# Attention scores on TensorE by row group: masks and product of one group in a row

## What is computed

```python
x = x + attention(layernorm(x), ctx, ctx, mask, ...)   # scores, softmax, values, wo
x = x + ffn(layernorm(x), ...)                          # router, top 2 of 8 experts, shared expert

scores = einsum('bhqd,bhkd->bhqk', Qh, Kh) / sqrt(8)
scores = where(causal or padding, -inf, scores)
probs  = softmax(scores, axis=-1)
```

## Time and profile before

| what | value |
|---|---|
| median of three runs | 856.8 us |
| lowest, highest | 856.01, 857.17 us |
| span of the profiled execution | 887.9 us |
| TensorE matmul, weight loads | 792.5 us (89%), 536.7 us (60%) |
| VectorE | 635.1 us (72%) |
| ScalarE | 638.0 us (72%) |
| GpSimd | 539.8 us (61%) |

### The profile page before, as it was taken

How to read it: one execution, slowest core, us unless ns; L and a number is a source line. 1 busy time by engine, 2 the same in 40 slices (tenths; PEclk the granted TensorE clock), 3 DMA queues, 4 the chain that set the end, 5 groups by cost and what they waited for, 6 DMA issues and landing times.

```text
span 887.9 us, 21709 instructions
## 1 busy us (share of the span) xinstructions
PE 792.5 (89%) x6977; PEld 536.7 (60%) x6977; DVE 635.1 (72%) x1774; ACT 638.0 (72%) x1185; POOL 539.8 (61%) x634
## 2 busy tenths in 40 slices
PE   5799999989999999999885747999999999967994
PEld 2355555545555555555454536888888888866773
DVE  5756667778687777856664547787777778756897
ACT  3478887877877777876596636988888888858730
POOL 6456665787878788776465743056666565644531
PEclk9899999999999999999898867999999999989998
DMA  4542643352222222211001113667777788773983
GB/s 123 163 141 86 201 127 112 108 164 60 68 72 74 65 74 82 68 59 49 29 20 58 46 69 110 240 218 257 249 246 262 248 293 288 269 227 108 249 232 106
DMA packets 100934, 126.97 MB, mean 143 GB/s; under 512 B 20919, under 2 KB 82039, under 8 KB 94807
## 3 DMA queue, kind: packets, MB, share of 16 engines
q1 hardware_dynamic: 92183, 107.08, 38.3%
q0 software_dynamic: 8640, 18.50, 5.9%
HBM read 77.84 MB, written 39.64 MB: 132 GB/s over the span
## 4 chain that ended last, share of the span: by engine, by line
PE 66%; DVE 9%; ACT 8%; issue 7%; another core or an unknown queue 4%; POOL 3%; SPq 1%; DMA 1%; ACTq 0%; DVEq 0%; POOLq 0%
PE bank L1344 8%; PE bank L1329 6%; ACT prob L760 5%; PE bank L1426 5%; PE bank L1424 5%; PE bank L1435 5%; PE bank L1437 5%; PE bank L1436 5%; PE bank L1425 5%; PE bank L1349 3%; PE bank L1361 3%; PE bank L1322 3%; PE bank L1443 2%; PE bank L1411 2%
## 5 line engine op out<-in xcount | busy, mean ns | idle before, releaser
L760 ACT ACTIVATE prob<-bank,padb,sc 120x512 f32<-120x512 f32 x256 | 178.1, 776 | 80.5 <-PE bank L1349 64.6
L1210 POOL DMA_INDIRECT y_scratch<-yo,ti x142 | 141.1, 993 | 131.2 <-DVE yo L1111 99.2
L1188 POOL TENSOR_SCALAR_AFFINE_SELECT prob<-prob 120x512 f32<-120x512 f32 x256 | 161.7, 635 | 86.2 <-ACT prob L760 80.6
L832 DVE TENSOR_REDUCE nm<-bank 128x4 f32<-128x480 f32 x256 | 150.2, 648 | 66.9 <-PE bank L1329 66.9
L1088 DVE TENSOR_TENSOR gl<-gf,gh 128x512 fp32r<-128x512 f32 (+1 forms) x220 | 144.3, 659 | 59.9 <-ACT gh L808 55.7
L1203 POOL DMA_INDIRECT xs_scratch<-x2r,idx x128 | 127.2, 993 | 49.9 <-issue 33.0
L808 ACT ACTIVATE gh<-gf 128x512 fp32r<-128x512 f32 (+1 forms) x220 | 132.5, 602 | 5.1
L1344 PE MATMUL bank<-qblk,kT 32*120 32x512 f32 x512 | 118.0, 650 | 0.1
L802 ACT ACTIVATE gf<-bank,wt 128x512 f32<-128x512 f32 (+1 forms) x156 | 99.7, 639 | 10.0 <-remote 5.6
L802 ACT ACTIVATE gf<-bank,shb 128x512 f32<-128x512 f32 x64 | 43.5, 679 | 47.0 <-DVE gl L1088 15.9
L1329 PE MATMUL bank<-kblk,qT 32*128 32x480 f32 x512 | 70.5, 616 | 0.7 <-DMA kblk<-kT 0.7
(11 more groups left out here) (202 smaller groups left out, 1653.3 us busy)
## 6 DMA issues: line engine op xcount, KB each, us to landing
wt<-w_scratch SPq DMA_DIRECT2D x39, 1032.0 KB
xt<-xs_scratch SPq DMA_DIRECT2D x32, 280.0 KB
w_scratch<-x2t SPq DMA_DIRECT2D x8, 1024.0 KB
wt<-y_scratch SPq DMA_DIRECT2D x28, 256.0 KB, 4.8
xs_scratch<-padc SPq DMA_DIRECT2D x15, 280.0 KB, 2.9
x<-in_x SPq DMA_DIRECT2D x16, 256.0 KB, 3.0
qblk<-qT SPq DMA_DIRECT2D x64, 64.0 KB
x_scratch<-x SPq DMA_DIRECT2D x16, 256.0 KB, 2.4
```

What stands on the lines that cost most here:

```text
L760: e.activation(prob[u % NP][0:LK, :], banks[bi][0:LK, :], ACT.Exp, scale=sc[0:LK, 0:1], bias=padb[0:LK, t:t + 1]).then_inc(a_ex, 1)
L832: e.tensor_reduce(nm[:, g, i // 2, :], bk[:, 0:480].rearrange("p (j k) -> p j k", j=4), AX.X, ALU.max, negate=True).then_inc(v_mx, 1)
L1188: e.affine_select(out=pv, in_=pv, compare_op=ALU.is_ge, fill=0.0, base=0, pattern=[[0, 4], [1, 128]], channel_multiplier=-1).then_inc(p_cu ...
L1210: e.indirect_dma_start(y_dram, bass.IndirectOffsetOnAxis(ap=ti_[r % NWS][:, c:c + 1], axis=0), yo_[r % NYO][:, c, :], None).then_inc(d_y[r ...
```

## The change

In A the loops over groups and over quarters of keys change places: a group's four mask matmuls follow its bank's wait, and its product follows them. The waits for the key blocks and for q stand after the first group's masks. In B a group's mask matmul comes first and its product second, and the wait for the spread maxima moves ahead of both. The matmul that opens a bank's sum and the one that closes it, with its count, change accordingly. Nothing else changes, the plan and the table of banks included.

```diff
-                    for c in range(4):
-                        for g, (b, had) in enumerate(taken):
-                            if c == 0:
-                                emptied(had)
+                    for g, (b, had) in enumerate(taken):
+                        emptied(had)
+                        for c in range(4):
                             e.matmul(banks[b][:, 0:480].rearrange("p (j k) -> p j k", j=4)[:, :, KB * c:KB * c + KB],
                                      causb[32 * g:32 * g + 32, c, :],
                                      mrow_[n % 2][32 * g:32 * g + 32, i, c, :].unsqueeze(1).to_broadcast([32, 4, KB]),
                                      start=(c == 0), stop=False, skip_group_check=True)
-                    e.wait_ge(d_kb[n % 2], 64 * (n // 2 + 1))
-                    e.wait_ge(a_Q, n + 1)
-                    for g, (b, _) in enumerate(taken):
+                        if g == 0:
+                            e.wait_ge(d_kb[n % 2], 64 * (n // 2 + 1))
+                            e.wait_ge(a_Q, n + 1)
                         e.matmul(banks[b][:, 0:480], qT_[n % 2][32 * g:32 * g + 32, 128 * i:128 * i + 128],
...
                 elif stage == "B":
                     e.wait_ge(d_qb[n % 2], 64 * (n // 2 + 1))
                     e.wait_ge(a_K, n + 1)
+                    e.wait_ge(v_nT, n + 1)
                     taken = bank_of[stage, n, i]
                     for g, (b, had) in enumerate(taken):
                         emptied(had)
+                        e.matmul(banks[b][0:LK, :], selb[32 * g:32 * g + 32, i, :],
+                                 nmT_[n % 2][32 * g:32 * g + 32, :, :].rearrange("p j q -> p (j q)"), start=True, stop=False,
+                                 skip_group_check=True)
                         e.matmul(banks[b][0:LK, :], kT_[n % 3][32 * g:32 * g + 32, LK * i:LK * i + LK],
-                                 qblk_[n % 2][32 * g:32 * g + 32, i, :, :].rearrange("p j q -> p (j q)"), start=True, stop=False,
-                                 skip_group_check=True)
-                    e.wait_ge(v_nT, n + 1)
-                    for g, (b, _) in enumerate(taken):
-                        e.matmul(banks[b][0:LK, :], selb[32 * g:32 * g + 32, i, :],
-                                 nmT_[n % 2][32 * g:32 * g + 32, :, :].rearrange("p j q -> p (j q)"), start=False, stop=True,
+                                 qblk_[n % 2][32 * g:32 * g + 32, i, :, :].rearrange("p j q -> p (j q)"), start=False, stop=True,
                                  skip_group_check=True).then_inc(m_B, 1)
```

## The result

The change made the kernel slower: 868.3 us median of 4 runs (867.5 to 871.8) against 856.4 of 4 runs of the kernel before (853.9 to 857.2), a ratio of 1.0139 (95% interval 1.0117 to 1.0161). An execution over 1.5% above the fastest of its kernel counts as slow and is left out of the ratios, which leaves only five of ten for the change with nb on GpSimd (all ten: 870.0 to 894.8 us) and two of four for three then one with short cuts, so these two ratios are weak.

The account below looks back on a forecast made before the run. A ring was taken to bind: B's exponentials free the next A's banks, A's maxima the next B's. Savings of 3.3 early, 5.1 steady and 1 at head and tail, scaled to 9, gave 848 us (range 842 to 854).

Parts of the forecast that it names:

- B: In B each group runs mask, half, half: first exponential 1.38 us after B's start, 0.24 or 1.74 us won.
- A's first product: First product in A waits only for its own masks, not the fourth bank; first maximum 0.15 to 0.40 us earlier.
- Early turn: Between 45 and 118 us a turn takes 6.11 us instead of 6.41: 3.3 us over 11 turns.
- Moved waits: B's wait for the transposed maxima and A's for kblk and qT stand elsewhere; costed at nothing.
- The sum: Early 3.3, steady 5.1, head and tail 1: 9.4 of the profiled 887.9 us, scaled and rounded to 9.
- two habits of TensorE: On TensorE, row groups start independently of each other, but completion is reported in program order.
- the period gets shorter by 0.96: Steady stretch, 118 to 400 us: each 53 us period of eight batches saves 0.96 us, 5.1 us in all.
- rival 2: Gain taken back elsewhere (VectorE's pauseless stretch, loads of x, low clock): same time, 855 to 858 us, chance 0.17.
- VectorE binds more than two turns in eight: Sign of a wrong forecast in the steady stretch, where two A per eight-batch period were taken to gain nothing.
- Issue: A's fourth group stands 36 instructions behind the first, formerly 6; taken at nothing, bounds 0 to 0.27 us per A.
- rival 1: A's fourth group starts too late because TensorE looks ahead too little: A ends 0.6 us late, 864 us, chance 0.17.
- The 47.8 us that ScalarE waits for B: ScalarE's idle time for B's last matmuls before its exponentials, 45 to 400 us, falls by 15 to 30 us.

Follow-up runs that it names:

- nb on GpSimd: The change plus L1194 planned earlier and nb (-mean x rstd) computed by GpSimd: 0.9902 of the kernel before; the kernel before with both edits 0.9963.
- three then one: B's new order, and in A groups 0 to 2 as before, then the fourth group's masks and product, against the kernel before: 1.0080.
- short cuts: GpSimd's causal cut (L1188) on one of four heads, 0.29 us instead of 0.63; against the kernel before: that kernel 0.9852, the change 0.9739.
- A alone: A's new order with B as before, against the kernel before: 1.0092.
- masks by group: The change, but in A all sixteen masks, group by group, stand ahead of the four products, against the kernel before: 1.0025.
- L1194 earlier: GpSimd's L1194 planned ahead of two row scatters; against the kernel before: that kernel 0.9948, the change 0.9965, masks by group 1.0033, three then one 1.0073.

## Why the prediction was wrong

**What held.** *B*: the exponentials follow by 1.32 (forecast 1.38), with a late fourth bank too. *A's first product*: 0.24 after A, and the first maximum 1.29 after the A at 62.43 (63.72; forecast 1.3). *Early turn*: 6.15 (forecast 6.11); over the eight turns from the ninth A it saved 2.5 us, where 3.3 were summed for eleven. *Moved waits*: none shows up as a cost. *The sum*: 9 us, measured as 9.6, give or take 5, once the cuts are short. How near the two are is luck: the measurement is too wide to test the terms, and it was made on another base. Of the two habits of TensorE, ends in order of the program held; starts free between groups held only within the limit below.

**What failed first: the step from "the first maximum comes earlier" to "the period gets shorter by 0.96".** I gave VectorE room (40.8 of 53 us busy), and asked where the ring binds, but only for the chain through TensorE, ScalarE and VectorE. GpSimd, fed by the same exponentials, was not in it. An exponential that comes earlier also frees a cut earlier, and that cut now starts before a small operation of VectorE instead of 0.27 us or more after it. The text names the principle of rival 2, a gain taken back elsewhere, and puts it at 855 to 858; I listed wider stretches of VectorE, loads and slices of low clock, and priced it as gain lost, never as loss. It was a loss: an operation of 0.15 us took up to 2.36, once or twice a period, with TensorE's pause and, in most cases, the halved clock behind it. Earlier exponentials are not the only way there: A alone, with B as before, met the cuts six times. A period, from one L922 to the second after it, is 57.5 us (248.55 to 306.01), where 52.0 was forecast and 53.0 was before (250.27 to 303.24). "VectorE binds more than two turns in eight" was a sign I named for being wrong, and it appeared: 14 of the 46 turns, 2.4 in eight, hold an L922 of over 1 us or come right behind one.

**What failed second: "Issue", taken at nothing.** The last half starts 1.09 after A, 0.39 later than free of waits before, over the 0.3 that I had given as the mark of rival 1. (That A's end moves was the other sign of being wrong.) That "a later end of A is covered in most turns" did not hold on this plan, where A's new order cost 1.1%. The bounds (0 to 0.27 us an A) did not hold it, since the price isn't one of instructions passed but of matmuls in a row for one group. Rival 1 had the effect on A, and 864 us, near the 868.3 by luck: its mechanism (a reach of TensorE counted in instructions) was wrong, and its lateness in every A is not what the time is made of, since with the cuts short the change gains its 9.6 us with the same 0.39.

**What also missed.** The 47.8 us that ScalarE waits for B did not fall by 15 to 30 but to 44.2. The wait is shorter each time (44.2 / 50 = 0.88, against 47.8 / 36 = 1.33) and there are more of them. With short cuts it falls from 61.3 us in 52 waits (before) to 47.6 in 56 (the change), by 13.7: nearly the forecast. So the row told something of the gain, but only against a base with the same cuts.

**How the loss divides.** Shown: with the cuts short nothing of the loss is left and there is a gain; with A's masks by group, on the plan as it was, 1.0139 becomes 1.0025. The two don't add. Not shown: what the stagger costs where VectorE isn't held (the only kernel with short cuts and less stagger, three then one, can't be told from the change), and by what way A's new order costs 10 us where VectorE is. Not settled either: what a given order and plan will meet. The rows of the table change their order from column to column, and I forecast it rightly for three then one on the old plan (1.000 to 1.010, measured 1.0080) and wrongly for both with L1194 earlier. Of the 22 L922 between 118 and 430 us in the change and in masks by group, 17 fit this: it gets in ahead of a cut whose exponential ended 0.12 us or less before that cut starts, and not where it ended 0.2 or more before. Two got in before a fourth cut that had long been ready (at 190.74 in the change), two waited for another operation of GpSimd (L1156), one met nothing. So this is a pattern and not a rule.

The Trainium skill (SBUF — State Buffer, Who interferes with whom) has a rule on this: VectorE and GpSimd share a pair of ports by a lock, held for the whole instruction, with the other one blocked. The rows agree (275.89: L922 ends 0.02 us behind the fourth cut). The section also names casts and scalings among the operations that can contend, in modes that use both pairs of ports, and here they waited as well (L882 2.20 us; L823 a median of 0.44 with three then one and 0.17 in its base). The rows add that four selects back to back could keep VectorE out for all four (2.36 us), though not always: with short cuts the L922 at 408.62 took 0.25 us beside four that started 0.25 us apart (408.57 to 409.59). By that rule one has to ask on which side of each cut every small SBUF operation of VectorE falls; no sentence of my prediction did.

## What to carry to other kernels

When an edit makes one engine's output come earlier, list everyone that it feeds, not only the next on the critical ring, and check the margin by which each now stands behind or ahead of a neighbour that it can block: here 0.27 us. Two kernels that differ in the order of work must be compared on more than one plan, or with the suspected collision taken away, before the order itself is judged: the change is 1.1% faster than its base with short cuts, and 1.4% slower with long ones. And where TensorE works on row groups side by side and they should start together, no more than four matmuls of one group should stand in a row; what that is worth in time depends on the rest, as three then one shows.

## What the runs showed of the hardware

- A small VectorE operation in SBUF, started while GpSimd's affine selects of 0.63 us ran back to back, took up to 2.36 us instead of 0.15. With selects of 0.29 us it took 0.15 to 0.25 in eleven of the twelve L922 between 118 and 430 us (the change with short cuts). The twelfth, 1.06 us, had another operation of GpSimd beside it.
- Row groups of TensorE start independently as long as few matmuls of one stand in a row: the next group started 0.01 us later for three, 0.015 for four, 0.07 for five and 0.13 for six. That a group can hold about three waiting matmuls, and that the next one for it stops all behind it, fits these four numbers; the depth itself wasn't measured.
- After a pause of 2.68 us TensorE's granted clock was 0.50 for the next 4.8 us, and a product of A that takes 1.02 to 1.03 us there took 1.92. In the first 460 us it was at that level for 55 us in the change, 27 in masks by group and 17 in before.
